# A four-layer graph network on one core: layer 3 moved into the batch norm's last loop, and row scales for 96 graphs made ahead of two seams

## What is computed

```python
h = relu(layernorm(x)); x = x + L0(h, adj)      # edge network, sums over neighbours
h = relu(layernorm(x)); x = x + L1(h, adj)      # three relu(adj @ (h @ W + b)), then @ Wout + bout
h = relu(layernorm(x))                          # layer 2
y = (adj @ h + h) @ weight + bias
y = y / max(norm(y, axis=2), 1e-12)             # per row
mean, var = masked mean and variance over all graphs and nodes, per feature
x = x + relu(((y - mean) / sqrt(var + eps) * gamma + beta) * mask)
h = relu(layernorm(x))                          # layer 3
x = x + tanh(concat(h, adj @ h) @ W1 + b1) @ W2 + b2
```

## Time and profile before

| what | us |
|---|---|
| median of three runs | 1465.61 |
| the profiled execution | 1463.7 |
| its span, first to last instruction | 1462.0 |
| TensorE matmul busy | 1316.5 |
| TensorE weight load busy | 1076.8 |
| VectorE busy | 1154.9 |
| ScalarE busy | 1105.1 |
| GpSimd busy | 502.5 |

### The profile page before, as it was taken

The page is one execution under the profiler, slowest core; times in us unless marked ns, Lnnn a source line. Parts: engine busy times, 40 slices in busy tenths (PEclk is TensorE's granted clock), DMA queues, the critical chain, the costliest instruction groups (busy, mean ns, idle before and its releaser), DMA issues. The chain is left out here.

```text
span 1462.0 us, 41154 instructions
## 1 busy us (share of the span) xinstructions
PE 1316.5 (90%) x11243; PEld 1076.8 (74%) x11244; DVE 1154.9 (79%) x2874; ACT 1105.1 (76%) x2426; POOL 502.5 (34%) x611
## 2 busy tenths in 40 slices
PE   3999999999999999999999999997999997972398
PEld 1777777877777777777777777875889887910298
DVE  7898988899888988889888998883444445978755
ACT  4788888888888888888888888863555555916676
POOL 1343344444443344444433444431222111066400
PEclk9999999999999999999999999997999998986599
DMA  7000000000000000000000000000000000000022
GB/s 154 22 10 9 8 7 14 7 7 7 7 14 7 7 7 14 7 7 7 7 14 7 7 7 7 0 2 1 0 0 0 0 0 0 0 1 0 4 54 57
DMA packets 40925, 18.11 MB, mean 12 GB/s; under 512 B 19572, under 2 KB 40886, under 8 KB 40886
## 3 DMA queue, kind: packets, MB, share of 16 engines
q1 hardware_dynamic: 40354, 17.42, 4.8%
q10 hardware_dynamic: 532, 0.21, 0.1%
HBM read 13.44 MB, written 4.19 MB: 12 GB/s over the span
## 5 line engine op out<-in xcount | busy, mean ns | idle before, releaser
L723 DVE SCALAR_TENSOR_TENSOR acc<-slot_banks,acc 128x768 f32<-128x768 f32 x512 | 487.7, 953 | 79.5 <-PE slot_banks L442 70.6
L792 POOL TENSOR_TENSOR acc<-acc 128x384 f32<-128x384 f32 x128 | 128.1, 1001 | 529.1 <-DVE onediff L717 420.3
L442 PE MATMUL slot_banks<-ac_hi,work 128*128 128x192 f16 x1408 | 265.3, 247 | 27.3 <-DVE work L705 26.1
L442 PE MATMUL slot_banks<-ac_lo,work 128*128 128x192 f16 x1408 | 264.1, 246 | 0.0
L442 PEld LDWEIGHTS slot_banks<-ac_hi,work 128*128 (+1 forms) x1408 | 137.4, 98 | 98.4 <-issue 76.1
L442 PE MATMUL slot_banks<-ac_hi,onediff 128*128 128x192 f16 x1024 | 183.1, 246 | 6.4 <-DVE acc L723 5.1
L442 PE MATMUL slot_banks<-ac_lo,onediff 128*128 128x192 f16 x1024 | 182.3, 246 | 0.0
L442 PEld LDWEIGHTS slot_banks<-ac_lo,work 128*128 (+1 forms) x1408 | 138.2, 98 | 20.2 <-issue 14.5
L778 POOL TENSOR_TENSOR ac_lo<-ac,ac_hi 128x384 f16<-128x384 f32 x128 | 123.1, 961 | 49.3 <-ACT ac_hi L582 49.3
L542 ACT ACTIVATE work<-bank 128x512 f16<-128x512 f32 x256 | 130.7, 601 | 1.2 <-PE bank L353 1.2
L705 DVE TENSOR_SCALAR work<-work,slot_key 128x1024 f16 x256 | 117.9, 480 | 12.2 <-issue 3.7
(11 more groups left out here) (261 smaller groups left out, 3291.4 us busy)
## 6 DMA issues: line engine op xcount, KB each, us to landing
adj_in<-in_adj_dram SPq DMA_DIRECT2D x32, 256.0 KB, 2.8
out_dram<-acc SPq DMA_DIRECT2D x32, 128.0 KB, 2.0
l1w<-in_L_gnn_W_dram SPq DMA_DIRECT2D x2, 64.0 KB
l1b<-in_L_gnn_b_dram SPq DMA_DIRECT2D x2, 64.0 KB
x_all<-in_x_dram SPq DMA_DIRECT2D x4, 0.2 KB, 11.8
nm_in<-in_nodemask_dram ACTq DMA_DIRECT2D x1, 64.0 KB
w1a<-in_L_gnn_W_dram ACTq DMA_DIRECT2D x1, 48.0 KB
w1b<-in_L_gnn_W_dram ACTq DMA_DIRECT2D x1, 48.0 KB
```

The costliest lines, as they stand in the source:

```text
L442: last = nc.tensor.matmul(unit(pair, t, 1), hot(t), part[:, q, H:2 * H].unsqueeze(1), start=False, stop=(e == 1 and (t % SB == SB - 1 or t ...
L723: nc.vector.scalar_tensor_tensor(out=sums, in0=unit((q + k) % 2, 0, SU), scalar=0.0, in1=sums, op0=ALU.min, op1=ALU.add).then_inc(s_free[k ...
L792: nc.gpsimd.tensor_tensor(acc[:, q, 0:2 * H], acc[:, q, 0:2 * H], acc[:, q, 2 * H:4 * H], ALU.add)
```

## The change

Three parts.

- **Layer 3 beside the final loop.** Layer 3's block is gone. TensorE's part of it stands in the batch norm's block behind the last reduction, with the same code, and so do SP's stores. VectorE has a new list, `fold_in`, and ScalarE a new one, `fold_in_act`, both written out step by step. They run the final loop `LEAD` = 6 chunks ahead of layer 3's steps. VectorE does the shift itself, adds every chunk to x itself, and makes the statistics straight after. GpSimd does none of the three.
- **Scales for 24 graphs at a time.** Three chunks make a batch (`QC` = 3, `NB` = 6 batches, the last of one chunk). `variances` is six operations on VectorE, the power -0.5 is one on GpSimd, and `scales` refines it with one step of Newton's method and makes `nmr`, four operations on VectorE. ScalarE's square root is not used for layer 3. Its tanh table is asked for ahead of the masked relus.
- **Layers 1 and 2.** 96 graphs' scales (`most`) are made ahead of each seam: for layer 1 in the steps of graphs 124 and 125 of layer 0, for layer 2 between the last two pairs of layer 1. The last 32 (`last_ones`) are made in the new block, on ScalarE behind the first eight normalisations.

```diff
+        most, last_ones = slice(0, 3 * B // 4), slice(3 * B // 4, B)
...
+                    if known(b) and b == B - GS + 1:
+                        layernorm_std(act, 3, most)
...
+                        if known(b) and b == B - GS:
+                            layernorm_var(dve, 3, most)
+                        if known(b) and b == B - GS + 1:
+                            layernorm_rstd(dve, 3, most)
...
-                layernorm_std(act, 3)
                 act.wait_ge(s_ln, 3)
                 for u in range(2):
                     for q in range(GS):
                         norm_h1(u, GS * u, q)
+                layernorm_std(act, 4, last_ones)
+                act.wait_ge(s_ln, 4)
...
+                layernorm_std(act, 5, most)
                 group_pair(NI - 1, False)
...
-                layernorm_scales(dve, 3)
+                layernorm_var(dve, 4, last_ones)
+                layernorm_rstd(dve, 4, last_ones)
...
-                with dve.Fori(1, NI) as i:
+                with dve.Fori(1, NI - 1) as i:
                     group_pair(i, i - 1)
+                dve.wait_ge(s_bn1, 3 * NI // 4)
+                layernorm_var(dve, 5, most)
+                layernorm_rstd(dve, 5, most)
+                group_pair(NI - 1, NI - 2)
...
-                layernorm_std(act, 4)
-                act.wait_ge(s_ln, 4)
+                act.wait_ge(s_ln, 5)
                 for u in range(2):
                     for q in range(GS):
                         norm_graph(s_hn2[u], u, GS * u, q, q == GS - 1)
+                layernorm_std(act, 6, last_ones)
+                act.wait_ge(s_ln, 6)
...
-                layernorm_scales(dve, 4)
+                layernorm_var(dve, 6, last_ones)
+                layernorm_rstd(dve, 6, last_ones)
```

More of the change, by code:

```diff
@@ new lines, in batch, with variances @@
+        def batch(k):
+            return slice(k * QC * GX, min((k + 1) * QC, NXC) * GX)
+        def variances(dve, k):
+            v = nc.vector
+            cols = batch(k)
+            m0, q0, m1, q1 = (bn6[:, cols, t] for t in (1, 2, 4, 5))
+            dve.wait_ge(s_bn2, min(QC * k + QC, NXC))
+            v.tensor_tensor(msum[:, cols], m0, m1, ALU.add)
+            v.tensor_tensor(var[:, cols], q0, q1, ALU.add)
+            v.tensor_tensor(dif[:, cols], m0, m1, ALU.subtract).then_inc(s_lnq, 1)
+            dve.wait_ge(s_lnq, 6 * k + 1)
+            v.tensor_scalar(var[:, cols], var[:, cols], 1.0 / F, EPS, ALU.mult, ALU.add)
+            v.scalar_tensor_tensor(out=dif[:, cols], in0=dif[:, cols], scalar=0.25, in1=dif[:, cols],
+                                   op0=ALU.mult, op1=ALU.mult).then_inc(s_lnq, 1)
+            dve.wait_ge(s_lnq, 6 * k + 2)
+            v.tensor_tensor(var[:, cols], var[:, cols], dif[:, cols], ALU.add).then_inc(s_lnq, 1)
@@ new lines, in scales @@
+        def scales(dve, k):
+            v = nc.vector
+            cols = batch(k)
+            root, error = std[:, cols], dif[:, cols]
+            dve.wait_ge(s_root, k + 1)
+            v.scalar_tensor_tensor(out=error, in0=root, scalar=-0.5, in1=root, op0=ALU.mult, op1=ALU.mult)             .then_inc(s_lnq, 1)
+            dve.wait_ge(s_lnq, 6 * k + 4)
+            v.tensor_tensor(error, error, var[:, cols], ALU.mult).then_inc(s_lnq, 1)
+            dve.wait_ge(s_lnq, 6 * k + 5)
+            v.scalar_tensor_tensor(out=rstd[:, cols], in0=error, scalar=1.5, in1=root, op0=ALU.add, op1=ALU.mult)             .then_inc(s_lnq, 1)
+            dve.wait_ge(s_lnq, 6 * k + 6)
+            v.scalar_tensor_tensor(out=nmr[:, cols], in0=msum[:, cols], scalar=-0.5, in1=rstd[:, cols],
+                                   op0=ALU.mult, op1=ALU.mult).then_inc(s_ln3, 1)
@@ L1579, in gnn_stack_kernel @@
-        s_out = [sem(f"stored{u}") for u in range(2)]
-        with nc.Block() as block:
-            @block.tensor
-            def _(pe):
                 def neighbours(i, u):
@@ L1668, in pair, with settled @@
-                def pair(i):
-                    for u in range(2):
-                        ahead, behind = following(i, u), preceding(i, u)
-                        if ahead is not None:
-                            copy_sums(*ahead)
-                        if behind is not None:
-                            update(*behind)
-                copy_sums(0, 0)
-                pairs(dve, pair)
-                update(NI - 1, 1)
+                steps = [0]
+                def settled(ins):
+                    steps[0] += 1
+                    ins.then_inc(s_vb, 1)
+                    dve.wait_ge(s_vb, steps[0])
@@ new lines, in _ @@
+                dve.wait_ge(s_var, 1)
+                settled(v.reciprocal(stat[:, 5, :], stat[:, 4, :]))
+                settled(v.tensor_tensor(stat[:, 5, :], stat[:, 5, :], gamma[:, :], ALU.mult))
+                fold_in(dve)
+            @block.scalar
+            def _(act):
+                act.activation(ss[:, :], ss[:, :], ACT.Sqrt).then_inc(s_nrm, 1)
+                for c in range(NXC):
+                    act.wait_ge(s_d[c % 2], c // 2 + 1)
+                    if c >= 2:
+                        act.wait_ge(s_dms, c - 1)
+                    act.activation(tmp[:, 2 + c % 2, :], yc(c), ACT.Square).then_inc(s_dq, 1)
+                act.wait_ge(s_vb, 5)
+                act.activation(stat[:, 4, :], stat[:, 3, :], ACT.Sqrt, bias=eps_col[:, 0:1]).then_inc(s_var, 1)
+                fold_in_act(act)
```

226 lines of the change are left out of this document (94 added, 132 removed).

## The result

The changed kernel takes 1448.19 us, the median of four runs (1447.9 to 1448.63); the kernel before took 1465.55 beside it (1463.8 to 1466.25). The ratio on record is 0.9892, with a 95% interval of 0.9875 to 0.9908; the quotient of the two medians is 0.9882. It is faster, as forecast, but by 17.4 us between the medians (15.8 by the ratio) where the sum said 11.9. The forecast of 1453.7 would be a ratio of 0.9919, just outside the interval.

A forecast was written before the change was run, and what follows sets the result against it. VectorE bounds the final loop, TensorE layer 3. Merged loop -11.1, power +2.0, seams -2.0 and -0.8 give -11.9: 1451.8 for the profiled execution, 1453.7 as median; range 1448.5 to 1459, to 1461.5 with the dear power.

The forecast's parts named there:

- The merged loop: Batch norm's final loop with layer 3: bound by VectorE while batch-norm work lasts, 123.3 us instead of 134.5, 11.1 less.
- Steps 1 to 8: Merged loop's mixed steps: 8 x 6.02 us plus three scales and two variances, 52.3 us, reaching 84.0.
- steps 11 to 14: Merged loop, layer 3 alone: 4 x 4.84 us, and 0.5 for the last scales, reaching 115.9.
- steps 9 and 10: Merged loop without scale-and-shift: 2 x 4.84 us, two variances and one scales, put at 12.0 us, reaching 96.0.
- The power: GpSimd's six powers in the merged loop: at most 1.6 us each, 0.33 each taken from VectorE, 2.0 us lost.
- powers over 1 us: Merged loop: a GpSimd power longer than this was listed as a sign that the prediction was wrong.
- The seam before layer 1: Early scales let ScalarE normalise at once: 3.4 us gained, 1.4 lost in layer 0's last group, net -2.0.
- The seam before layer 2: Between layer 1's last pairs: 3.4 us gained, 2.6 lost by TensorE's wait, net -0.8, without the gap's clock effect.
- Rival 1: Merged loop: powers take 1.6 us each, all on VectorE, 9.6 instead of 2.0, giving 1461.3; chance 0.12.
- Rival 2: Mixed steps: TensorE, 74% busy, loses its clock in half of eleven steps, 16 us, giving 1469.7; chance 0.10.
- Rival 3: Merged loop: the two loops don't overlap, steps cost 7.57 us instead of 6.57, giving 1464.7; chance 0.06.
- The table load: Tanh table load of 1.28 us, moved ahead of the relus into ScalarE's 3.39 us wait, costs nothing.

The follow-up runs named there:

- no_shift: The changed kernel without the batch norm's shift (the addition of beta left out, so the output lacks that term): 1438.42 us, ratio 0.9822.
- seam1_only: The kernel before with only the early scales of 96 graphs in layer 0's steps of graphs 124 and 125 added: 1461.51 us, ratio 0.9984.
- seam2_only: The kernel before with only the scales of 96 graphs ahead of layer 2's seam added: 1464.31 us, ratio 1.0009.
- power_doubled: The changed kernel with GpSimd computing five of the six powers a second time into a spare tile: 1448.49 us, ratio 0.9903.
- shift_on_gpsimd: The changed kernel with all 16 shifts given back to GpSimd in the merged loop: 1453.82 us, ratio 0.9936.
- merge_only: The changed kernel with both early batches of scales, for layers 1 and 2, undone: 1453.24 us, ratio 0.9919.
- seam2_hidden: The changed kernel with the 96-column work ahead of layer 2 moved to where VectorE and ScalarE idle in layer 1's last pair: 1443.15 us, ratio 0.9861.
- no_seam2: The changed kernel without the early scales of 96 graphs ahead of layer 2's seam: 1448.57 us, ratio 0.9897.
- seam2_warm: The changed kernel with eight small unused matmuls on TensorE while it waits in layer 1's last pair: 1444.54 us, ratio 0.9868.

## Why the prediction was right, and where it was short

- **The merged loop, right in mechanism and in the price of a step.** I had 6.02 us for a plain step and it is 5.99, bound by VectorE as `no_shift` shows; with a third of a batch it is 6.56 in the mean of three (5.99, 6.97, 6.73) for my 6.57. The first copy comes 1349.21 - 1325.34 = 23.87 us after the first scale, predicted 23.7. Steps 1 to 8 took 52.1, predicted 52.3. The loop is 121.6 us against my 123.3. Of the 1.7, about 0.5 is at the second copy, 1.34 us behind the first where I took 2.09 from a slow TensorE, and 0.9 at steps 11 to 14: 18.95 for 19.9, because TensorE was ahead of VectorE when the mixed steps ended, and the last scales fell into its steps. Two slips of adding are in the sum: steps 9 and 10 come to 12.2 and not 12.0 (they took 11.8), and 134.5 - 123.3 is 11.2 and not 11.1.
- **The power, wrong in both numbers.** I bounded it by 1.6 us and it takes 4.16; I put 2.0 us of port on VectorE and there is none. The errors didn't touch because VectorE asks for the result later than 4.16 us: variances at 1337.33, their use at 1344.33. My own sign of failure, "powers over 1 us", would have misled me. This term and the 1.7 are why the loop brought 12.9 us in the trace and not 9.1.
- **The seam before layer 1.** Opening to first normalisation was 3.4 us and is nothing. The work in layer 0's last group cost 0.9 and not 1.4: against the same fold of graph 123, at 971.50 before and 970.51 now, the changed kernel is 0.99 us ahead, and after the two steps 0.10 (995.38 and 995.28). Net -2.5 for -2.0. `seam1_only` measures -2.3 (0.9 to 3.8). The profile shows 4.7, because layer 0's last stretch, from that last fold to the block's opening, took 9.15 us for 10.36. That isn't the change's: `seam2_only`, which doesn't touch layer 0, has 9.06.
- **The seam before layer 2, the term that failed by its clock.** The wait is 2.29 us for 2.6, the gain 3.4 as said. I left out "what the gap does to the clock" and named it only for the range; it is 3.0 us in this trace and 1.5 in three others with the same code. Net +1.9 or +0.4, where I had -0.8.
- **Rival 1, the power dear**, is refuted by `power_doubled`, in spite of a power dearer than I allowed. **Rival 2, TensorE loses its clock in the mixed steps**, is refuted for this kernel by the windows: 1.00 over 53.3 us. Its premise was off too: TensorE is 88% busy there where I reckoned 74%, and why its busy time in a step grew was not looked into. The Trainium skill's warning (TensorE: Matmul & The Clock Gate, "A second HAM failure mode: psum-queue depth-cycling") that small idles between groups of matmuls can make the clock swing did not show in this loop. Waits of 3.43 us in the same loop, in `shift_on_gpsimd`, did bring 0.50. What the change itself cost of the clock it cost in layer 1's last pair. **Rival 3** is refuted: VectorE has no gap in a mixed step.
- **The table load** is hidden as I said: it begins at 1324.41, ahead of the first scale, and takes 1.28 us.

The forecast gave 3.8 us too little for the loop and 0.5 for layer 1's seam, and 1.2 to 2.7 too much for layer 2's, so the errors cancel in part; without that the time would lie further out at the low end of my range. By the runs then: some -12 for the loop, -2.3 for layer 1's seam, and for layer 2's between -1 and +4; the whole, by ratio, is 0.0108 x 1465.6 = 15.8 us. The rest up to the medians' 17.4 lies within what the kernel before varies by between executions.

## What to carry to other kernels

Small work put ahead of a seam gains most where its engines idle. Here, where a matmul waited for it, it cost that wait and then a stretch at half clock, 2.3 and 1.5 to 3.0 us for a seam of 3.4. Before moving an elementwise operation to GpSimd, ask which VectorE operation will stand beside it and what is ahead of it in GpSimd's queue: all 16 shifts there lost 5.6 us in one order, and nine of them gained 5.5 in another. And when two loops with different bounds are merged, add up the busier engine's starts from rows of each; that gave the step within 0.03 us.

## What the runs showed of the hardware that I had not expected

- GpSimd's power of 128x24 takes 4.16 us, of 128x8 1.64, and stretches nothing on VectorE, while its two-input add of 128x512 stretches a two-input add on VectorE from 0.41 to 1.11 us, and neither statistics nor a copy out of PSUM.
- The slow stretch at layer 1's start differs between executions: from the first normalisation to the last pair's first copy (less the 2.3 us stall where there is one) it took 201.4 to 201.6 us in the kernel before, the changed one, `merge_only`, `no_shift` and `shift_on_gpsimd`, and 198.5 to 199.4 in `seam2_hidden`, `no_seam2`, `seam2_only`, `seam2_warm`, `power_doubled` and `seam1_only`. The part of the batch norm between row roots and first scale took either 42.8 to 43.1 or 44.9 to 45.5. Neither goes with an edit: `power_doubled` has the changed kernel's code in both places and differs from it in both (198.8 for 201.5, 45.0 for 43.0). So a difference of 2 or 3 us between two single profiles tells nothing by itself. What decides it was not tried.
- Matmuls of 128 columns, issued while TensorE waits at a border, keep the granted clock up: 1.00 where it was 0.77 at layer 1's start (15 ahead of the border and 6 behind it) and 0.57 at layer 2's (11 and 5), and 0.81 for 0.52 ahead of layer 3 (10).
